# Splitting the second expert layer's weights inside the first layer's expert loop, in a two-layer vision tower on one Trainium2 core

## The reference

```python
# layer 0
toks = x[token_idx]
def mlp(w1e, w2e):
    return jax.nn.gelu(toks @ w1e) @ w2e
ys = jax.vmap(mlp)(w1, w2)
...
out = jnp.zeros((N, D), dtype=inputs.dtype).at[token_idx].add(res)
# layer 1
h = jax.nn.relu(jnp.einsum('td,ehd->teh', xf, W1) + b1)
y = jnp.einsum('teh,edh->ted', h, W2) + b2
moe = jnp.einsum('te,ted->td', gates, y)
sh = jax.nn.relu(xf @ sW1.T + sb1) @ sW2.T + sb2
out = moe + 0.1 * K * sh
```

## Time and profile before

| what | value |
| --- | --- |
| median of 3 runs | 1279.76 us (1279.2 to 1281.05) |
| the profiled execution's own time | 1276.82 us |
| its span, first to last instruction | 1275.0 us |
| mean granted TensorE clock | 0.712 |
| busy over the span | TensorE 61%, VectorE 65%, ScalarE 45%, GpSimd 22% |
| setup block of layer 1 | 932.8 to 1024.0 us |
| loop block of layer 0, first to last matmul | 564.8 to 713.2 us |

### The profile page before, as it was taken

The page is one execution under the profiler, slowest core; times in us unless marked ns, Lnnn a source line. Parts: engine busy times, 40 slices in busy tenths (PEclk is TensorE's granted clock), DMA queues, the critical chain, the costliest instruction groups (busy, mean ns, idle before and its releaser), DMA issues. The chain is left out here.

```text
span 1275.0 us, 21332 instructions
## 1 busy us (share of the span) xinstructions
PE 772.0 (61%) x6936; PEld 544.6 (43%) x6937; DVE 829.4 (65%) x1545; ACT 578.7 (45%) x1073; POOL 286.1 (22%) x226
## 2 busy tenths in 40 slices
PE   3726682444299302039999578757622259699993
PEld 2524230111176201029997343224422126599972
DVE  4677797999598778845454277947768853154531
ACT  1236000888587314416554153058735155177651
POOL 6500005000000000016776302100000000267751
PEclk9658555555598655559999787555565579899997
DMA  7500200000063006533433210000037110233332
GB/s 237 179 19 25 56 19 13 13 19 6 26 224 105 1 4 222 174 98 48 60 57 49 64 43 1 1 6 2 1 115 248 39 44 1 71 50 59 58 46 62
DMA packets 49018, 81.74 MB, mean 64 GB/s; under 512 B 8412, under 2 KB 37800, under 8 KB 48916
## 3 DMA queue, kind: packets, MB, share of 16 engines
q1 hardware_dynamic: 32564, 64.27, 15.5%
q0 software_dynamic: 16384, 16.53, 8.4%
HBM read 64.71 MB, written 17.50 MB: 64 GB/s over the span
## 5 line engine op out<-in xcount | busy, mean ns | idle before, releaser
L649 PE MATMUL a_pp<-a_qkb 16*128 16x256 bf16 x384 | 98.5, 410 | 107.7 <-DVE a_v L765 72.5
L1608 PE MATMUL m_pu<-m_xgT,m_w 128*128 128x256 f16 (+1 forms) x1380 | 157.0, 263 | 5.8 <-DVE m_xgT L1709 3.0
L1565 POOL DMA_INDIRECT m_xg<-xn_d,m_token x78 | 78.0, 1000 | 308.4 <-POOLq L1776 175.5
L1573 POOL DMA_INDIRECT h_d<-m_yo,m_token x78 | 124.1, 1591 | 78.6 <-DVE m_yo L1727 56.1
L1608 PEld LDWEIGHTS m_pu<-m_xgT,m_w 128*128 x1380 | 127.4, 99 | 30.1 <-issue 9.4
L1624 PE MATMUL m_py<-m_w,m_hT 128*128 x1404 | 125.8, 246 | 2.3 <-DVE m_yo L1727 1.8
L1709 DVE COPY m_xgT<-m_px 128x768 f16<-128x768 f16 (+1 forms) x46 | 22.8, 497 | 143.7 <-PE m_px L1598 143.7
L1624 PEld LDWEIGHTS m_py<-m_w,m_hT 128*128 128x128 f16 x1404 | 111.6, 98 | 10.3 <-issue 5.0
L649 PEld LDWEIGHTS a_pp<-a_qkb 16*128 16x128 bf16 x384 | 40.6, 126 | 165.4 <-DVE a_v L765 92.7
L741 ACT ACTIVATE a_ex<-a_v,a_nb 128x256 bf16 (+1 forms) x192 | 95.0, 495 | 34.2 <-DVE a_nb L783 32.6
L1717 DVE SCALAR_TENSOR_TENSOR m_hT<-m_pu,m_unit,m_hT 128x512 f16<-128x512 f32 (+1 forms) x138 | 85.8, 662 | 18.4 <-ACT m_hT L1673 18.3
(11 more groups left out here) (380 smaller groups left out, 1574.4 us busy)
## 6 DMA issues: line engine op xcount, KB each, us to landing
m_stage<-in_m_w SPq DMA_DIRECT2D x16, 768.0 KB, 5.5
m_stage<-in_m_w SPq DMA_DIRECT2D x16, 576.0 KB, 5.5
tokw_stage<-in_m_w SPq DMA_DIRECT2D x8, 768.0 KB, 5.6
a0w_stage<-in_m_w SPq DMA_DIRECT2D x8, 768.0 KB, 4.4
tokw_stage<-in_m_w SPq DMA_DIRECT2D x8, 576.0 KB, 4.7
a0w_stage<-in_m_w SPq DMA_DIRECT2D x8, 576.0 KB, 3.8
a_qkb<-qk_d SPq DMA_DIRECT2D x16, 192.0 KB, 3.3
xn_d<-m_x SPq DMA_DIRECT2D x8, 384.0 KB, 4.0
```

Source lines behind the costliest of these rows:

```text
L649: last = nc.tensor.matmul(pp[:, j, k, qt, :], qkb[:, par, h, qt * P:(qt + 1) * P], qkb[:, par, H + h, :], start=True, stop=True)
L1565: pool.indirect_dma_start(xg[:, m % 2, j, :], None, xn_d, bass.IndirectOffsetOnAxis(ap=token[:, n:n + 1], axis=0)).then_inc(got[m % 2], 16)
L1573: pool.indirect_dma_start(h_d, bass.IndirectOffsetOnAxis(ap=token[:, n:n + 1], axis=0), yo[:, m % 2, j, :], None, compute_op=ALU.add).then ...
L1608: last = nc.tensor.matmul(pu[:, u, q // 2, (q % 2) * w:(q % 2 + 1) * w], w1e[:, wpart, tail * FF + q * P:tail * FF + (q + 1) * P], xgT[:, ...
```

## The change

While the loop of layer 0 runs, the weights of layer 1 are now fetched, split, and written back to memory as halves (`w1h`, `w2h`, new scratch tensors). Each of the 16 large steps takes one piece: ScalarE makes its high half at the end of its part of the step (`next_high`), VectorE its low half behind `result` (`next_low`). SP's program has, behind `load_next`, two fetches, and then for each piece n: wait for low half n, store both halves (`keep`), fetch piece n + 2. There are two buffers (`raw`, `parts`), one for first and one for second matrices, so piece n + 2 uses what piece n used. The setup of layer 1 no longer splits anything: SP loads the 16 pairs of halves into `w1` and `w2` behind its stores of `xn_d` and waits for all of them at the block's end. Layer 0's own setup is as before.

```diff
@@ setup block @@
-            PIECES = 2 * E
+            PIECES = 0 if layer else 2 * E
+            def load_halves(sp, e):
+                for down, dst in enumerate((w1, w2)):
+                    w = WIDTH[down]
+                    sp.dma_start(dst[:, :, e * w:(e + 1) * w],
+                                 scratch["w2h" if down else "w1h"][e].rearrange("p (r w) -> p r w", r=2))\
+                      .then_inc(ready, 16)
...
+                    if layer:
+                        for e in range(E):
+                            load_halves(sp, e)
+                        sp.wait_ge(ready, 16 * 2 * E)
                     sp.wait_ge(stored, 64)
@@ loop block @@
+            def next_high(act, i, u):
+                w = NEXT_WIDTH[u]
+                act.wait_ge(fetched[u], i * 16 + 16)
+                if not isinstance(i, int) or i > 0:
+                    act.wait_ge(put[u], i * 16)
+                act.activation(parts[:, u, 0, 0:w], raw[:, u, 0:w], ACT.Identity, scale=NEXT_SCALE[u])\
+                   .then_inc(split_high, 1)
+
+            def next_low(dve, i, u):
+                w = NEXT_WIDTH[u]
+                dve.wait_ge(split_high, i * 2 + u + 1)
+                nc.vector.scalar_tensor_tensor(parts[:, u, 1, 0:w], raw[:, u, 0:w], NEXT_SCALE[u], parts[:, u, 0, 0:w],
+                                               ALU.mult, ALU.subtract).then_inc(split_low, 1)
...
                         load_next(sp, ahead)
+                        fetch(sp, 0)
+                        fetch(sp, 1)
+                        for n in range(2 * E):
+                            keep(sp, n)
+                            if n + 2 < 2 * E:
+                                fetch(sp, n + 2)
...
                         high_half(2)
+                        if not layer and large(i, u):
+                            next_high(act, i, u)
...
                         result(i, u)
+                        if not layer and large(i, u):
+                            next_low(dve, i, u)
```

More of the change, by code:

```diff
@@ L1174, in experts @@
         with ExitStack() as s1:
-            stage = c.sb(f"{L}_stage", [P, 4, W], F32, s1)
+            stage = None if layer else c.sb(f"{L}_stage", [P, 4, W], F32, s1)
             xn = c.sb(f"{L}_xn", [P, NT, D], F32, s1)
@@ L1223, in experts @@
             stage_in = [c.sem(f"{L}_stage_in{b}") for b in range(4)]
-            high, low, loaded = (c.sem(f"{L}_{n}") for n in ("high", "low", "loaded"))
+            high, low, loaded, ready = (c.sem(f"{L}_{n}") for n in ("high", "low", "loaded", "ready"))
             (spread, rooted, normed, xhigh, xlow, turned, kept_a, kept_v, stored, rsplit, scored, chain, leveled,
@@ L1244, in piece @@
                         (up_scale, down_scale)[down])
+            def load_halves(sp, e):
[4 more added lines that the diff above has]
+                      .then_inc(ready, 16)
             def load_piece(sp, n):
+                if n >= PIECES:
+                    return
                 if n >= 4:
@@ L1527, in experts, with fetch, keep @@
             yo = c.sb(f"{L}_yo", [P, 2, 2, D], F32, s1)
+            if not layer:
+                raw = c.sb(f"{L}_raw", [P, 2, W], F32, s1)
+                parts = c.sb(f"{L}_parts", [P, 2, 2, W], F16, s1)
+                fetched, put = ((c.sem(f"{L}f_{n}0"), c.sem(f"{L}f_{n}1")) for n in ("fetched", "put"))
+                split_high, split_low = c.sem(f"{L}f_split_high"), c.sem(f"{L}f_split_low")
+            NEXT_WIDTH = (W, FC * D)
+            NEXT_SCALE = (c.scale[:, 2:3], c.scale[:, 3:4])
+            def next_high(act, i, u):
[10 more added lines that the diff above has]
+                                               ALU.mult, ALU.subtract).then_inc(split_low, 1)
+            def fetch(sp, n):
+                w = NEXT_WIDTH[n % 2]
+                sp.dma_start(raw[:, n % 2, 0:w], a["m1_w2" if n % 2 else "m1_w1"][n // 2]).then_inc(fetched[n % 2], 16)
+            def keep(sp, n):
+                w = NEXT_WIDTH[n % 2]
+                sp.wait_ge(split_low, n + 1)
+                sp.dma_start(scratch["w2h" if n % 2 else "w1h"][n // 2].rearrange("p (r w) -> p r w", r=2),
+                             parts[:, n % 2, :, 0:w]).then_inc(put[n % 2], 16)
             pu = c.ps(f"{L}_pu", [P, 2, 3, 512], F32, s1)
@@ L1556, in _ @@
                         load_next(sp, ahead)
+                        fetch(sp, 0)
[4 more added lines that the diff above has]
+                                fetch(sp, n + 2)
+                        for u in range(2):
+                            sp.wait_ge(put[u], 16 * E)
                         sp.wait_ge(ahead, next_count)
@@ L2590, in layout @@
     return {k: np.ascontiguousarray(v) for k, v in f.items()}
[L2593 removed]
+SCRATCH = {"qk": ((2 * D, T), BF16), "xn": ((T + 2 * P, 2 * D), F16), "h": ((T + 2 * P, D), F32),
+           "w1h": ((E, P, 4 * FF), F16), "w2h": ((E, P, 2 * FC * D), F16)}
 def kernel(**inputs):
```

## The result

| what | before | after |
| --- | --- | --- |
| median, 20 runs each on the same chip | 1277.41 us (1271.63 to 1281.05) | 1284.03 us (1275.27 to 1288.16) |
| ratio | | 1.005 [1.0033, 1.0067] |
| span of the profiled execution | 1275.0 us | 1282.1 us |
| loop block of layer 0, first transpose to last `down` | 148.4 us | 184.0 us |
| setup block of layer 1 | 91.2 us | 64.4 us |

The change made the kernel 0.5% slower, where I had forecast 0.4% faster. The setup gave back 26.8 us, the loop took 35.6 us more, and the rest of the program moved by -1.7; that is the 7.1 us between the spans. 1284 lies inside the range of 1261 to 1289, but only because that range also covered a loss; the change went the other way than I had forecast.

The account below looks back on a forecast made before the run. No single engine bounds the kernel; TensorE sets layer 0's loop, VectorE's line layer 1's setup. Loop +21.0 (+23.4 less about 2.4) and setup -26.6 give -5.6 us: 1274 us against the median, range 1261 to 1289.

Parts of the forecast that it names:

- The setup: Layer 1's setup: five savings along VectorE's line, 3.55 + 6.1 + 9.8 + 4.5 + 2.6 = 26.6 us.
- Rival 3: Layer 1's setup: halves loaded in shorter rows land late, setup ends 6 us later; about 0, 1280 us; chance 0.06.
- The ring of fetch and store: Layer 0's loop: fetch, ScalarE's and VectorE's work and store set the pace, 16.5 us per two steps instead of 13.16.
- L: Layer 0's loop: time from a piece's finished low half until the fetch two pieces on has landed; taken as 7.7 us.
- the prediction's own formula: Layer 0's loop changes by 7 x (L - 4.36) - 2.4 us; the whole kernel by that less 26.6.
- How large is L?: Layer 0's store and fetch: 6.3 us undisturbed, 8.9 with all GpSimd traffic in the way; about half taken, 7.7.
- As work, both fit: Layer 0's loop: ScalarE's 1.57 us fits its gap of 2.49, VectorE's 1.82 its gap of 2.86.
- short fall: Layer 0's loop: a brief drop of TensorE's clock costs nothing, with 3.4 us spare per pair of steps.
- rival 4: Layer 0's loop: TensorE's clock drops behind idle time, at most 69 us; chance 0.04 that it costs over 5 us.
- Rival 1: Layer 0's loop: transfers nearly hidden; 1264 us at L = 6.3, 1253 if all hidden; chance 0.16.
- Rival 2: Layer 0's loop: SP's store and fetch, slowed behind GpSimd's traffic, lose more than setup gains; 1283 at L = 8.9; chance 0.22.
- The condition at the prediction's end: Layer 0's loop: forecast called wrong if GpSimd's indirect transfers land late and TensorE waits for gathered rows; no size or chance.

Follow-up runs that it names:

- h5: Changed kernel with gathers issued ahead of the adding stores and VectorE's low half cut into four instructions: 0.9873 of before, loop 162.9 us.
- g2: e1 with VectorE's low half cut into four instructions: 0.9807 of before, loop 151.1 us.
- e1: Changed kernel, but from the third piece on SyncE fetches and stores only 16 of 1536 columns: 0.9915 of before, loop 161.6 us.
- h1: Changed kernel with only VectorE's low half cut into four instructions: 0.9939 of before, 1268.1 us, loop 165.3.
- e3: Changed kernel, from the third piece on with both SyncE's transfers and VectorE's low half at 16 columns: 0.9828 of before, loop 152.5 us.
- e2: Changed kernel, but from the third piece on VectorE makes only 16 columns of the low half, transfers whole: 0.9978 of before, loop 176.0 us.
- h2: Changed kernel, but from the third piece on SyncE stores only 16 of 1536 columns, fetches whole: 0.9978 of before, loop 170.2 us.
- h3: Changed kernel, but from the third piece on SyncE fetches only 16 of 1536 columns, stores whole: 1.0008 of before, loop 172.9 us.
- g1: Changed kernel with SyncE's rows cut to 1,536 and 768 bytes, same bytes, store in two transfers: 1.0126 of before, loop 191.3 us.
- f3: Changed kernel, gathers ahead of adding stores, low halves one step earlier: runs at 1248.0 to 1249.1 and 1286.0 to 1291.2 us; 0.9787 for the first group.
- f6: f3 with the low half in four instructions: 0.9836 of before; repeated, 0.9803 for three runs, three more at 1320.9 to 1327.2 us.

## Why the prediction was wrong

**The setup was right, term by term.** 26.6 us foretold, 26.8 measured. The waits came where they were placed: 0.28 at the square root, 0.70 ahead of the scores, 3.38 behind the list matmuls. Between the same instructions before and after, VectorE's line lost 15.9 us from the reciprocal to L1410 (foretold 6.1 + 9.8), 4.5 from there to L1430 (4.5), and 2.75 from there to L1511 (2.6). The last load left at 1004.5 and none of these loads took over 14.5 us, so all had landed by 1019, 11 us before the block's end. Rival 3 did not happen.

**The ring of fetch and store is real, but L was taken too long, and it was not what bound the loop.** L was 6.6 us in the step shown and 6.3 on average, the "undisturbed" value and not the 7.7 that I chose. By the prediction's own formula even 6.6 makes 7 x (6.6 - 4.36) - 2.4 = +13.3 us of loop and -13 in all. The loop took +35.6. The pairs of steps were 18 us on average, longer than 8.8 + 6.6 = 15.4. Where the gathers were in time (h5), the ring showed itself, with 15.5 us a pair against 16.5 in the sum.

**The step that failed** is the one under "How large is L?", that GpSimd's transfers can only make SyncE's slower ("At best none of it is in the way (6.3), at worst all of one step's (8.9)"). I asked what GpSimd's traffic does to SyncE, and not what the added work does to GpSimd. So the sum has only ScalarE's ring, 16.5 us a pair, where the ring through GpSimd's gathers and TensorE's `down` set the pace at 18. What the sum left out:

- *GpSimd is held for one instruction of VectorE.* The step "As work, both fit" counted VectorE's 1.82 us in a gap of 2.86 as free. That gap lies just where GpSimd issues its stores and gathers. Cutting the instruction gave back 10.5 us with small transfers (g2 against e1) and 18.7 with whole ones (h1); leaving it out gave 9.1 and 8.0 (e3, e2), so the holding itself is worth some 8 to 10 us, and the rest of h1's gain is open. The Trainium skill has a lock of this kind, in "SBUF — State Buffer", section "SBUF: two separate sides": VectorE and GpSimd share a port pair as an exclusive lock, and GpSimd can't write the descriptors of its transfers while a VectorE instruction in a 2-port mode has it. The same section says of a VectorE instruction with two inputs from SBUF, as this one, that it takes the lock only against a GpSimd instruction that reads SBUF. The issues here (2.95 for 1.62 and 2.02 for 0.98 us, each ending one undisturbed issue after VectorE's instruction) look like it; that a `scalar_tensor_tensor` from float32 and float16 to float16 delays them is what the runs add. That it is this lock they do not show.
- *Gathers land late beside SyncE's bytes.* 6.5 us at the worst instead of 4.1, with 0.6 us to spare. They do so also when GpSimd isn't held (e2). Both transfers count, by about half each (h2, h3), and shorter rows did not help (g1). With the gathers a step earlier and the low half cut (h5) the waits are back near the value of before. Why a gather takes longer, queueing or something else, these runs don't tell.
- *The clock.* Behind five of the six waits of 3.0 to 4.0 us TensorE's granted clock fell (to 0.57 over the `down` behind the first), and `down` took 4.25 to 5.64 instead of 3.13 us; behind the sixth it did not fall, and `down` took 3.21. In all TensorE was busy 13.3 us longer, the "short fall" that rival 4 had at nothing, since it assumed TensorE to have time to spare. `down` stands in the second ring, so the time was not spare. With the waits gone in f3, busy time is at 143.9.

**The rivals.** Rival 1 needed what L in fact was (6.3), and its 1264 did not come. Rival 2 had the sign and nearly the number (1283 at L = 8.9), but that is luck: its mechanism, a slower pair of store and fetch, did not happen. By the Trainium skill's rule in "DMA: Bandwidth & Descriptors", section "Queues, rings and completion order", I had put the loss in SyncE's queue, with L = 8.9; the trace, with 6.3, does not agree with what I made of the rule. Rival 4 named a cost that came, 13.3 us where over 5 had a chance of 0.04. The condition at the prediction's end, gathers landing late and TensorE waiting for them, is what happened; I had it as a sign of error and gave it no price and no chance.

**What stays open.** The second group of times comes where the gathers are ahead and the low halves early (f3, f6: 7 of 24 runs), not in h5 (0 of 5) nor in h1 (0 of 8). No execution of the upper group was profiled, so its cause is unknown. Open too are the part of h1's gain that e2 doesn't give, and why a gather lands late. The runs were read by one profiled execution each.

## What to carry to other kernels

Before work is put into a VectorE gap, look at what GpSimd issues in that gap: here a single long instruction held up the indirect transfers whose issue fell into it, by up to 1.3 us of its 1.81, and cutting it in four was worth more than it cost. Follow each engine's order once round: a gather that stands behind a store which waits for the result closes a ring, and the time that it has to spare is what any new delay eats first. Price a new stream of transfers not only by its own landing, but by what it does to those whose landing someone waits for, and give these more lead before adding it. When an idle gap of TensorE is foreseen, add the matmuls that will run behind it at the lower clock.

## What the runs showed of the hardware

- A `scalar_tensor_tensor` of 128 x 1536 (1.81 us) held up the issue of an indirect transfer to its end: 2.95 instead of 1.62 us for an adding store; one of 128 x 1152 (1.41 us) made a gather's 2.02 instead of 0.98 us.
- Four instructions instead of one cost VectorE 2.20 instead of 1.81 us, and in g2 GpSimd's store took 1.75 us beside them. GpSimd does not always get in between: a gather beside four took 2.56 us in h5, and an adding store 2.94 in f6.
- Cutting SyncE's rows to a quarter made its 768 KB fetch 8.1 us instead of 5.9 and did not speed up the gathers beside it (5.6 us in the median, 3.1 with whole rows).
- A loop with the DMA engines at 0.75 of their time, 204 GB/s, ran as fast in its profiled execution (148.3 us, f3) as one at 0.35 and 55 GB/s (148.4), where every transfer had lead enough.
